# Second attention phase: who issues the row transfers of the maxima, and when

## What is computed

```python
x = x + _L0_attn_a_ref(_layernorm(x), ...)
x = x + _L0_ffn_ref(_layernorm(x), ...)
x = x + _L0_attn_b_ref(_layernorm(x), ...)   # 32 heads of 16, causal, softmax(q k^T / 4) v
x = x + _L0_ffn_ref(_layernorm(x), ...)
```

## Time and profile before

| | us |
|---|---|
| median of 3 runs | 1956.14 (1955.39 to 1958.18) |
| the profiled execution | 1951.68 |
| its span, first to last instruction | 1949.9 |
| TensorE busy (share of the span) | 1658.7 (85%) |
| VectorE busy | 1099.6 (56%) |
| ScalarE busy | 861.1 (44%) |
| GpSimd busy | 650.3 (33%) |
| second attention phase, pairs only | 978 to 1574 |

### The profile page before, as it was taken

One profiled execution on the slowest core, in us unless ns is written; L12 is line 12 of the kernel. 1 busy time (PEld: TensorE's weight loads), 2 busy tenths in 40 slices (PEclk: granted clock), 3 DMA queues, 4 the chain that ended last, 5 costly groups with the idle time before them and its releaser, 6 DMA issues. The chain is left out here.

```text
span 1949.9 us, 31436 instructions
## 1 busy us (share of the span) xinstructions
PE 1658.7 (85%) x10544; PEld 1157.8 (59%) x10544; DVE 1099.6 (56%) x2394; ACT 861.1 (44%) x1514; POOL 650.3 (33%) x1926
## 2 busy tenths in 40 slices
PE   4888988989857999998288798798888857999997
PEld 4555655656535787786155475465555435777785
DVE  5777676676627654543555645644644527654543
ACT  3456555565524544532334433443443425454541
POOL 4455455454421221311224433433432412221211
PEclk8899999999997999999589898999889988999999
DMA  2000000001016311010534433633453226311010
GB/s 99 2 20 17 34 24 24 24 2 34 13 56 187 94 60 65 0 44 22 154 38 54 68 60 52 87 45 66 59 64 66 35 69 181 92 54 65 0 44 22
DMA packets 78118, 106.95 MB, mean 55 GB/s; under 512 B 13194, under 2 KB 49674, under 8 KB 77972
## 3 DMA queue, kind: packets, MB, share of 16 engines
q1 hardware_dynamic: 77972, 105.10, 24.1%
HBM read 62.34 MB, written 16.78 MB: 41 GB/s over the span
## 5 line engine op out<-in xcount | busy, mean ns | idle before, releaser
L247 PE MATMUL f_ring<-f_xt,f_codes 128*128 128x512 f32 (+1 forms) x1408 | 360.6, 399 | 6.6 <-DVEq L1539 5.5
L247 PEld LDWEIGHTS f_ring<-f_xt,f_codes 128*128 128x128 f32 (+1 forms) x1408 | 263.7, 188 | 76.0 <-DVEq L1539 6.2
L1397 POOL TENSOR_TENSOR f_ht<-f_work,f_ht 128x512 fp32r<-128x512 f32 (+1 forms) x88 | 114.6, 1306 | 472.9 <-ACT f_ht L1457 472.9
L834 ACT ACTIVATE ab_region<-ab_scores 128x512 f32<-128x512 f32 x320 | 181.0, 600 | 144.3 <-PE ab_scores L1122 144.2
L691 POOL TENSOR_SCALAR_AFFINE_SELECT ab_region<-ab_region 128x128 f32<-128x128 f32 x512 | 140.3, 298 | 240.5 <-ACT ab_region L834 240.2
L834 ACT ACTIVATE aa_region<-aa_scores 128x512 f32<-128x512 f32 x320 | 184.5, 599 | 81.3 <-PE aa_scores L1122 78.5
L1550 DVE TENSOR_TENSOR f_work<-f_ring,f_work 128x512 f32<-128x512 f32 (+1 forms) x176 | 120.6, 689 | 146.1 <-ACT f_work L1446 117.3
L1446 ACT ACTIVATE f_work<-f_ring,f_scales 128x512 f32<-128x512 f32 (+1 forms) x176 | 120.8, 686 | 171.7 <-PE f_ring L247 171.3
L1122 PE MATMUL ab_scores<-ab_stacks 99*128 99x512 bf16 (+3 forms) x512 | 135.4, 328 | 69.8 <-DMA ab_stacks<-ab_rowparts 66.8
L247 PE MATMUL f_ring<-f_dcodes,f_ht 128*128 128x512 f32 (+1 forms) x704 | 176.0, 404 | 10.3 <-DVE f_down_x L1520 9.3
L691 POOL TENSOR_SCALAR_AFFINE_SELECT aa_region<-aa_region 128x128 f32<-128x128 f32 x512 | 137.6, 299 | 88.5 <-ACT aa_region L834 88.0
(11 more groups left out here) (181 smaller groups left out, 2962.2 us busy)
## 6 DMA issues: line engine op xcount, KB each, us to landing
ab_stacks<-ab_parted SPq DMA_DIRECT2D x192, 128.0 KB, 5.6
f_x<-mid SPq DMA_DIRECT2D x32, 256.0 KB, 4.2
f_raw<-mid SPq DMA_DIRECT2D x32, 256.0 KB, 4.2
f_raw<-in_gate_q SPq DMA_DIRECT2D x10, 512.0 KB, 6.6
f_raw<-in_up_q SPq DMA_DIRECT2D x10, 512.0 KB, 4.9
f_raw<-in_down_q SPq DMA_DIRECT2D x10, 512.0 KB, 3.7
aa_x<-in_x SPq DMA_DIRECT2D x16, 256.0 KB, 2.8
aa_res<-in_x SPq DMA_DIRECT2D x16, 256.0 KB, 2.7
```

The lines of the kernel that those rows point to most:

```text
L247: mm = pe.matmul(out, w, x, start=start and i == 0, stop=stop and i == len(pairs) - 1)
L834: act.activation(probs[:, s // 2 % 2, SUB * (s % 2) + i, :], scores[:, sbk, :], ACT.Exp, scale=0.25).then_inc(scores_freed[sbk].sem, 1)
L1397: pool.tensor_tensor(ht[0:r, LO, n, :], hid[0:r, n % 2, :], ht[0:r, HI, n, :].bitcast(F32), ALU.subtract).then_inc(hid_lo.sem, 1)
```

## The change

`max_rows` is now a function of the engine that issues. In the first attention phase, and for the very first pair of the second, SyncE issues as before. In the second phase all other row transfers (63 of 64) are issued by ScalarE, on its own queue, right behind the exponential of i = 3 in its program (`ROWS_AT + 1`); SyncE no longer waits for the copied rows there. The wait for the copied rows moves to ScalarE with the transfer. Nothing else changes: neither the data, nor the copies, nor the waits of TensorE.

```diff
--- before.py
+++ after.py
@@ -560,6 +560,13 @@
 
         block = ctx.enter_context(nc.Block())
 
+        def max_rows(eng, b, s):
+
+            eng.wait_ge(rows_copied.sem, rows_copied.at(b, s + 1))
+            h, _, _ = heads(s, 0)
+            eng.dma_start(stacks[MAXROW:MAXROW + 3, unit(s) % 2, h:h + 2, :],
+                         rowparts[MAXROW:MAXROW + 24, :]).then_inc(rows_made.sem, 16)
+
         def whole(eng, part):
 
             part(table.head, ("head", 0), 0)
@@ -598,13 +605,6 @@
             for t in range(XB):
                 load(1, t)
 
-            def max_rows(b, s):
-
-                sp.wait_ge(rows_copied.sem, rows_copied.at(b, s + 1))
-                h, _, _ = heads(s, 0)
-                sp.dma_start(stacks[MAXROW:MAXROW + 3, unit(s) % 2, h:h + 2, :],
-                             rowparts[MAXROW:MAXROW + 24, :]).then_inc(rows_made.sem, 16)
-
             def residual(b, t):
 
                 sp.wait_ge(stored[t % 2].sem, stored[t % 2].at(b, 16 * (t // 2)))
@@ -619,8 +619,8 @@
                 for pos, step in enumerate(region[0]):
                     if step is not None:
                         bs, s, i = step
-                        if i == ROWS_AT and (after := following(region, b0 + bs, s, 1)) is not None:
-                            max_rows(*after)
+                        if rope and i == ROWS_AT and (after := following(region, b0 + bs, s, 1)) is not None:
+                            max_rows(sp, *after)
                     for kind, bb, u, _ in table.started(region, pos, 2, "Q", "K"):
                         regroup(b0 + bb, u, QK.index(kind), (0,))
                     for kind, bb, u, _ in table.started(region, pos, 3, "Q", "K"):
@@ -640,7 +640,7 @@
                         if t + 2 < NT:
                             residual(b0 + bb, t + 2)
                     if step is None and region is table.head and region[0][pos + 1] is not None:
-                        max_rows(0, 0)
+                        max_rows(sp, 0, 0)
 
             def regroup(b, u, a, parts):
 
@@ -833,6 +833,8 @@
                         act.wait_ge(scores_filled[sbk].sem, scores_filled[sbk].at(b, nth + 1))
                         act.activation(probs[:, s // 2 % 2, SUB * (s % 2) + i, :], scores[:, sbk, :], ACT.Exp,
                                        scale=0.25).then_inc(scores_freed[sbk].sem, 1)
+                        if not rope and i == ROWS_AT + 1 and (after := following(region, b, s, 1)) is not None:
+                            max_rows(act, *after)
                     for kind, bb, u, _ in table.started(region, pos, 2, "Q", "K"):
                         a = QK.index(kind)
                         banks.emptied(act, where, (kind, u, 0, 0))
```

## The result

The change makes the kernel slower, by 0.3%: median 1965.0 us against 1958.97 for the kernel before in the same series (20 runs each), ratio 1.0027 with a 95% interval of 1.0016 to 1.0038. The forecast was 17.7 us faster; measured are 5 to 6 us slower. That 1965.0 lies inside the wide range of 1930 to 1968 says nothing for the forecast: the upper half of that range was there for its rivals.

A forecast was written before the change was run, and what follows sets the result against it. TensorE, waiting for row transfers, was taken to bound the phase. Gains 22.0 + 6.6 + 2.0 less 10.7 and 2.2 made 17.7 us: 1938.4 us median, 1934.0 for a profiled execution; own range 1930 to 1946, wide range 1930 to 1968.

The forecast's parts named there:

- What bounds the phase: Second attention phase: TensorE sets the pace, standing 66.8 us for row transfers; behind long waits the build is equally late.
- The builds start earlier, and so end earlier: SyncE's twelve 128 KB copies per build: start without the wait for copied rows, the whole train moving by 2.37 us.
- my two terms for it: Waits around builds: eight long stalls shortened by 2.37 us each, and three short ones, together 6.6 us.
- builds no earlier: Rival: the build's last parts set its end, so only 0.38 x 11 = 4 is won; 1965 us, chance 0.07.
- The first scores ahead of the wait: Scores of i = 0 at eight long stalls: run inside the stall instead of after it, 0.38 us each.
- the new wait of the maxima: Sign at L1082: TensorE's maxima wait for the builds, 8 stalls of about 4.2 us, about 34.
- Late issue, per wait: Thirteen short waits: ScalarE issues behind the fourth exponential, 0.82 us later each, 10.7 us lost.
- Company on the DMA engines: Row transfers at s = 1, 5, 9, 13, issued mid-build: wait for one 128 KB copy, 1.09 us; 2.2 us lost.
- the 2.8 that I had named as a sign of being wrong: Sign: the prediction is wrong if rows issued within a build take over 2.8 us to be used.
- one line for both: Rival: ScalarE's transfers line up behind what SyncE has queued; net 14 us slower, 1970 us, chance 0.12.
- The clock: TensorE after stalls: three short stalls nearly vanish and partly keep the clock, 2.0 us gained, bounds 0 and 8.7.
- the clock falling in the thirteen grown short gaps: Rival: gaps grown from 0.38 to 1.2 us lower TensorE's clock, 2.9 us each, 38 in all; 1976 us, chance 0.04.

The follow-up runs named there:

- the kernel with i = 2 on ScalarE: The changed kernel with ScalarE issuing the row transfer one step earlier, behind the exponential of i = 2: 1936.0 us, 0.9887 of the kernel before.
- The half with these transfers alone: The kernel before, with ScalarE issuing only row transfers with no build in flight (s = 0, 3, 4, 7 and so on), SyncE the rest: 1968.73 us, ratio 1.0052.
- that half of the change with i = 3 in a build: The kernel before, with ScalarE issuing only the row transfers of s = 1, 5, 9, 13, behind the exponential of i = 3: 1953.25 us, ratio 0.9974.

## Why the prediction was wrong, point by point

**What bounds the phase** was right: TensorE's wait for the rows, and behind it the build. But not all came through that wait: in the profiled execution of after it is 1.3 us shorter than before, while the phase is 5.0 longer.

**The builds start earlier, and so end earlier**: right, 2.34 us earlier (0.03 behind the cast instead of 2.37), and as long as before, about 15.3 us from start to last landing. The stall of s = 6 in the second batch fell from 6.90 to 4.76 in the kernel with i = 2 on ScalarE. That kernel is worth 22 us in all, where my two terms for it were 8 x 2.37 + 6.6 = 25.6. The rival "builds no earlier" is out; that its price, 1965, is the measured time is chance.

**The first scores ahead of the wait** (0.38 x 8 = 3.0): wrong, 0. It needed the rows to overtake the build, and on no queue did they. The rows stayed the last to come at every long stall, so the new wait of the maxima that I named as a sign never showed. I had treated a queue of its own as a way of its own; what had to be asked was where two queues meet.

**Late issue, per wait**: right in mechanism and size. I took the issue 0.1 us behind the start of the exponential, measured is 0.01, and the short wait grew by 0.76 (0.39 to 1.15) against 0.82. The count was wrong: I priced the thirteen pairs that waited already and gave the others slack from one odd pair. At three pairs s = 4 with output projections between steps 2 and 3 the slack was the distance from step 2 to step 3 itself; moving the issue behind step 3 took it away and made three new waits of 1.13. The half with these transfers alone costs 10 us; the term was 10.7. That the two are so near is luck: a wrong count met a somewhat smaller price for each.

**Company on the DMA engines** (2.2 us): this is the step that failed. I let a transfer wait for one copy, 1.09 us; it waits for all that were issued before it, and costs 17 us. From issue to use it was 5.24 instead of 2.05, three copies' worth more and far over the 2.8 that I had named as a sign of being wrong, and the 0.78 of slack became a stall of 2.0 at all but one odd pair that opens behind a build's start, 4.2 in the first. The price, by the medians: the kernel with i = 2 gains 22 us, that half of the change with i = 3 in a build gains 5; the difference, 17 us (0.9974 - 0.9887 of 1959), is what the lateness in a build costs. The traces place most of it. In this phase the profiled execution of the change is 24.4 us longer than that of the kernel with i = 2: 11.6 in the short waits, 7.2 in the in-build ones, 3.7 in TensorE's own time (506.2 against 502.5) and 2.6 in its wait for GpSimd's split. The last three make 13.5; the rest of the 17 I can't place. That some of it would be absorbed at s = 5 was right (2.19 and 0.99 above). The rival "one line for both" was the true mechanism; its 3.3 us per stall was too high for all but the first, since a transfer with six copies issued ahead finds one of them landed, and its price, with 14 slower, too.

The Trainium skill states both sides of this (DMA: Bandwidth & Descriptors, "Queues, rings and completion order"). One rule there is that each DMA engine turns between queues, packet by packet. The trace doesn't show that this brings a 6 KB transfer ahead of 128 KB copies: the packets of ScalarE's queue begin when the copies issued before them have been moved (six, with 0.79 MB, in the lines above), and those of GpSimd's at 11.7 of twelve. Another rule of that section is that a semaphore's increment from a DMA engine lands only after all earlier writes of that engine, across its queues. By that rule, the data may be early and only the signal late. The trace agrees with the second half: in a build 2.37 us pass from the first packet to the use, against 0.74 with nothing ahead. But the data is not early either: it comes 2.87 us behind the issue instead of 1.37. So the lateness has two parts of like size, 1.5 us until the packets move and 1.6 until they count. What makes the order, the engines or something ahead of them, no run here shows.

**The clock** (2.0): no gain shows; TensorE is busy 3.8 us longer for the same matmuls in the profiled execution of after, with the clock down in 14 stretches instead of 11. That was one of my signs of being wrong, and it came. The rival as I wrote it, the clock falling in the thirteen grown short gaps, is out: it fell behind none of them. It fell behind seven of the fifteen in-build stalls, and this cost is part of the 17 us. How much of the 3.8 is the clock's, one execution of each kernel can't say.

**The sum in measured terms**: 22 gained by the early builds, 10 lost by the late issue where nothing is queued, 17 lost by it inside the builds: 5 us slower, measured 5 to 6. (The 17 is worked out from the half that gains 5, so this sum tests only that the two halves add up.) Against the forecast that is 6.6 less gained (28.6 in two terms), no 2.0 of the clock, and 14.8 more lost by company.

The faster version is a by-product: the builds' first copies ahead of the wait on SyncE, or ScalarE's issue one step earlier, each at 0.989 of the kernel before.

## What to carry to other kernels

A transfer moved to another engine's queue leaves the first engine's program, but here it kept its place in the line for the DMA engines. Count the bytes issued before it, whoever issued them, and place a small urgent transfer by when it is issued. When a wait is taken off an engine that issues many transfers, look first at what that engine issues next: putting this ahead of the wait, on the same queue, gave the whole gain here. Slack must be taken from every kind of pair, not from one. And where a semaphore comes late, the record of the packets tells whether the data was late too.

## What the runs showed of the hardware

A row transfer takes 0.73 us of ScalarE's queue, as of SyncE's (0.70 to 0.75), but it starts beside the exponential ahead of it: 0.01 us behind its start (1225.42 and 1225.43), or even before it when the cast ahead is still running (issue at 1235.76, exponential at 1236.00). The next exponential then starts 0.79 behind the last instead of 0.49.

With the DMA engines full of 128 KB copies, a 6 KB transfer from ScalarE took 5.24 us from issue to use, and 2.11 with nothing ahead. Its packets began 2.87 us behind the issue instead of 1.37, in the order of issue over both queues, and from the first packet to the use it took 2.37 instead of 0.74. With an eighth of the bytes in as many copies and packets it no longer waited.

Behind a stall of 1.99 us TensorE's clock was 0.51 for 3 us; behind a wait of 1.14 us it stayed at 1.00. It did not fall behind each stall of 2 us: in the phase after it fell behind seven of fifteen stalls of 1.3 to 4.2 us.
